# Moving the branch product of a stream-mixing layer from the autocorrelation's period into the last part of the kernel

## What is computed

```python
x_norm = x * jax.lax.rsqrt(jnp.mean(x * x, axis=-1, keepdims=True) + RMS_EPS)
H_res_logits = (x_norm @ W_res.T).reshape(B, T, n, n) + H_res_base
H_pre_logits = x_norm @ W_pre.T + H_pre_base
H_post_logits = x_norm @ W_post.T + H_post_base
H_res = sinkhorn_log(H_res_logits)          # 50 iterations on 4 x 4
H_pre = jax.nn.softmax(H_pre_logits, axis=-1)
H_post = jax.nn.softmax(H_post_logits, axis=-1)
H_res = (1.0 - g) * I + g * H_res
x_streams = x.reshape(B, T, n, C)
x_pre = jnp.einsum('btnc,btn->btc', x_streams, H_pre)
y = x_pre @ W_branch
x_mixed = jnp.einsum('btij,btjc->btic', H_res, x_streams)
y_distributed = jnp.einsum('btc,btn->btnc', y, H_post)
return (x_mixed + y_distributed).reshape(B, T, nC)
```

## Time and profile before

| | us |
|---|---|
| median of 3 runs | 1248.21 (1247.65 to 1251.31) |
| the profiled execution | 1247.06 |
| its span | 1245.1 |
| the last part (mixing_phase), in the span | from about 1109.4 |
| PE busy | 1029.9 (83%) |
| DVE busy | 932.4 (75%) |
| ACT busy | 641.3 (52%) |
| POOL busy | 492.4 (40%) |
| table loads of ACT | 25 in all, 1.28 each |

### The profile page before, as it was taken

How to read it: one execution, slowest core, us unless ns; L and a number is a source line. 1 busy time by engine, 2 the same in 40 slices (tenths; PEclk the granted TensorE clock), 3 DMA queues, 4 the chain that set the end, 5 groups by cost and what they waited for, 6 DMA issues and landing times. The chain is left out here.

```text
span 1245.1 us, 23491 instructions
## 1 busy us (share of the span) xinstructions
PE 1029.9 (83%) x7928; PEld 781.0 (63%) x7928; DVE 932.4 (75%) x2818; ACT 641.3 (52%) x1827; POOL 492.4 (40%) x684
## 2 busy tenths in 40 slices
PE   5699999999999999999648999999887995615056
PEld 4577777787777777777436677767665663313034
DVE  6766787666678666666507778779998998897994
ACT  6434555544455544445516677778567655323133
POOL 2523443333343333344324666666565542201020
PEclk9799999999999999999679999999999997657578
DMA  9011011111101111110132123223222211139025
GB/s 377 25 42 57 19 57 57 57 57 40 45 28 57 57 57 57 40 41 19 58 120 85 68 83 117 89 77 123 73 81 81 73 39 38 43 120 332 0 56 131
DMA packets 47235, 95.72 MB, mean 77 GB/s; under 512 B 5952, under 2 KB 30400, under 8 KB 47168
## 3 DMA queue, kind: packets, MB, share of 16 engines
q1 hardware_dynamic: 47168, 94.91, 22.9%
HBM read 64.48 MB, written 27.26 MB: 74 GB/s over the span
## 5 line engine op out<-in xcount | busy, mean ns | idle before, releaser
L613 POOL TENSOR_TENSOR prob_G<-prob_G,rl 128x512 f32<-128x512 f32 x96 | 99.8, 1040 | 258.2 <-DVE rl L501 258.2
L383 ACT ACTIVATE prob_G<-prob_G,negm 128x128 f32<-128x128 f32 x384 | 148.8, 389 | 89.5 <-DVE negm L443 89.5
L244 PE MATMUL ps_qkv<-w_hi,xT_hi 128*128 128x512 f32 x384 | 156.7, 408 | 13.5 <-DVE prob_G L506 8.6
L245 PE MATMUL ps_qkv<-w_lo,xT_hi 128*128 128x512 f32 x384 | 151.4, 394 | 0.0
L246 PE MATMUL ps_qkv<-w_hi,xT_lo 128*128 128x512 f32 x384 | 151.2, 394 | 0.0
L316 PE MATMUL ps_qkv<-wo_hi,aT_hi 128*128 128x512 f32 x256 | 107.7, 421 | 0.0
L318 PE MATMUL ps_qkv<-wo_hi,aT_lo 128*128 128x512 f32 x256 | 102.1, 399 | 0.0
L317 PE MATMUL ps_qkv<-wo_lo,aT_hi 128*128 128x512 f32 x256 | 101.9, 398 | 0.0
L244 PEld LDWEIGHTS ps_qkv<-w_hi,xT_hi 128*128 128x128 f32 x384 | 73.2, 191 | 39.0 <-issue 16.1
L439 DVE TENSOR_TENSOR prob_G<-ps_s,mask 128x512 f32<-128x512 f32 x96 | 65.0, 677 | 41.4 <-PE ps_s L227 40.8
L468 DVE TENSOR_TENSOR xT_lo<-ps_t,xT_hi 128x512 fp32r<-128x512 f32 x16 | 11.1, 693 | 104.2 <-ACT xT_hi L422 104.2
(11 more groups left out here) (246 smaller groups left out, 2819.6 us busy)
## 6 DMA issues: line engine op xcount, KB each, us to landing
xin<-in_x SPq DMA_DIRECT2D x16, 512.0 KB, 3.3
xres<-in_x SPq DMA_DIRECT2D x16, 512.0 KB, 5.0
x<-xres SPq DMA_DIRECT2D x16, 512.0 KB, 2.6
c_xin<-x SPq DMA_DIRECT2D x16, 512.0 KB, 4.9
c_cin<-in_ctx SPq DMA_DIRECT2D x16, 512.0 KB, 4.2
c_b_xres<-x SPq DMA_DIRECT2D x16, 512.0 KB, 3.3
rows_x<-c_row SPq DMA_DIRECT2D x64, 128.0 KB, 2.3
m_xm<-rows_x SPq DMA_DIRECT2D x16, 512.0 KB, 8.6
```

Of the source, the lines that this page charges most:

```text
L244: nc.tensor.matmul(ps_qkv[:, n, :], xT_hi[:, k, :], w_hi[:, k, cols], start=k == 0, stop=False)
L245: nc.tensor.matmul(ps_qkv[:, n, :], xT_hi[:, k, :], w_lo[:, k, cols], start=False, stop=False)
L383: r = nc.scalar.activation(prob(g)[:, j, :], prob(g)[:, j, :], ACT.Exp, bias=negm[:, h:h + 1], accum_out=lsum[:, h:h + 1])
L613: nc.gpsimd.tensor_tensor(prob(g), prob(g), rl[:, g * GROUP:(g + 1) * GROUP].rearrange("p (j o) -> p j o", o=1).to_broadcast([P, GROUP, T] ...
```

## The change

In the period of the autocorrelation the maxima, exponentials, reciprocals, the weighted sum, its transposes, the branch product and body 17 go; rows_x is sent as soon as x3 is there, and rows_y is not used. Chains b and c stand at steps 96 and 8, not 126 and 16, when the last part begins. In the last part DVE does the softmax of all 16 rows at once, on 128 x 16 x 8 values, between the steps of the chains, with one exponential on ACT. PE spreads the pre shares and the means (early), ACT copies them, and POOL builds diagonal tiles for all rows in four operations (pre_diag). Then a row's branch is eight products of 128x128 parts of the row with 32-column diagonal tiles, which give the transposed weighted sum, a copy by ACT, two products with W_branch, and a copy by ACT into ym. Branches of rows 0 to 4 come before chain a's output, those of rows 5 to 15 after it. At the kernel's start ACT asks for one table set that holds exponential and logarithm. The diff, cut:

```diff
 def attention_phase(...):
...
         def _(act):
+            nc.scalar.preload_act_table_set("natural_log_exp_and_others")
             act.wait_ge(const_in, 48)
...
 def advance(dve, chain, to, most=1000):
...
-        if k > 1:
+        if k == 1:
+            dve.wait_ge(chain.logits_done, chain.first_row + chain.n)
+        else:
             dve.wait_ge(chain.step, k - 1)
...
 def autocorrelation_phase(...):
...
-                         (15, 4): ((one_b, 56),), (16, 0): ((one_b, 88),), (16, 3): ((one_c, 2),), (16, 4): ((one_b, 100), (one_c, 6)),
-                         (17, 0): ((one_b, 116),), (17, 4): ((one_b, 126), (one_c, 16))})
+                         (15, 4): ((one_b, 56),), (16, 0): ((one_b, 86),), (16, 3): ((one_c, 2),), (16, 4): ((one_b, 96), (one_c, 8))})
...
-            body(B + 1, 1, near=False, far=False, last=False, tail=True, ahead=False)
...
-                if tail:
-                    sp.wait_ge(y_done, b - 1)
+                if last:
+                    sp.wait_ge(x3_done, b)
...
-                    sp.dma_start(rows_y[b - 2], row[par][:, D:ROW]).then_inc(row_out[par], 16)
...
-                    for i in range(2):
-                        r = nc.tensor.transpose(xpT_at[:, i * T:(i + 1) * T], xp[:, i * P:(i + 1) * P], idf[:])
-                    r.then_inc(xpT_ps, 1)
...
-                        r = nc.tensor.matmul(y_ps_at, xpT[:, i, :], wb_sb[:, i, :], start=i == 0, stop=i == 1)
...
-                    nc.scalar.activation(he[:], fact(b - 1, 1 - par, AT_PRE, NS), ACT.Exp, bias=hx[:, 0:1],
-                                         accum_out=hs[:, 0:1]).then_inc(he_done, 1)
...
-                        nc.vector.scalar_tensor_tensor(xp[:], x[:, n * C:(n + 1) * C], he[:, n:n + 1], xp[:], ALU.mult, ALU.add).then_inc(xp_step, 1)
...
 def mixing_phase(...):
...
+        pre_parts = ((0, 5), (5, 9), (9, 13), (13, 16))
...
         def _(pe):
             pe.wait_ge(const_in, 32)
+            pe.wait_ge(share_step, SHARES)
+            for g in range(NS):
+                r = nc.tensor.matmul(p_sel[:, g, 0:B * EARLY], sel_sb[:, g, :],
+                                     early[:, :, :].rearrange("p b k -> p (b k)"), start=True, stop=True)
+            r.then_inc(early_ps, 1)
+
+            def branch(n):
+                if n == 0:
+                    pe.wait_ge(wb_in, 16)
+                pe.wait_ge(pre_diag_done, 1 + max(i for i, (first, _) in enumerate(pre_parts) if n >= first))
+                if n > 0:
+                    pe.wait_ge(pre_done, n)
+                for h in range(2):
+                    for g in range(NS):
+                        r = nc.tensor.matmul(p_pre[:, h * T + g * W:h * T + (g + 1) * W], xm[n][:, g, h * P:(h + 1) * P],
+                                             pre_diag[:, n * NS + g, :], start=True, stop=True)
+                r.then_inc(pre_ps, 1)
+                pe.wait_ge(pre_done, n + 1)
+                if n > 0:
+                    pe.wait_ge(y_done, n)
+                for h in range(2):
+                    r = nc.tensor.matmul(p_y[:, 0:C], xpT[:, h, :], wb_sb[:, h, :], start=h == 0, stop=h == 1)
+                r.then_inc(y_ps, 1)
+
             for chain in chains:
...
+                if chain is not one_c:
+                    for c in chains[group(chain):(group(chain) + 1 if chain is one_a else len(chains))]:
+                        pe.wait_ge(rows_in[group(c)], 16 * c.n)
+                        for n in range(c.first_row, c.first_row + c.n):
+                            branch(n)
                 pe.wait_ge(coef_step, COEFS * (group(chain) + 1))
...
         def _(act):
...
+            def branch(first, to):
+                for n in range(first, to):
+                    act.wait_ge(pre_ps, n + 1)
+                    if n > 0:
+                        act.wait_ge(y_ps, n)
+                    nc.scalar.activation(xpT[:, :, :], p_pre[:, 0:2 * T].rearrange("p (h t) -> p h t", h=2), ACT.Copy).then_inc(pre_done, 1)
+                    act.wait_ge(y_ps, n + 1)
+                    nc.scalar.activation(ym[n][:], p_y[:, 0:C], ACT.Copy).then_inc(y_done, 1)
...
+            branch(0, 2)
+            logs(one_b, FIRST_LOGS + 1, FIRST_LOGS + BLOCK_LOGS)
+            branch(2, one_a.n)
             copies(one_a)
-            take_out(0, 2)
-            logs(one_b, FIRST_LOGS + 1, FIRST_LOGS + BLOCK_LOGS)
-            take_out(2, one_a.n)
+            take_out(0, one_a.n)
+            branch(one_b.first_row, one_b.first_row + 3)
             logs(one_c, FIRST_LOGS + 1, FIRST_LOGS + BLOCK_LOGS)
+            branch(one_b.first_row + 3, B)
             logs(one_b, FIRST_LOGS + BLOCK_LOGS + 1, FIRST_LOGS + 2 * BLOCK_LOGS)
...
         def _(pool):
             pool.wait_ge(const_in, 32)
+            pool.wait_ge(early_done, EARLY)
+            for first, to in pre_parts:
+                wide = [P, (to - first) * NS, W]
+                nc.gpsimd.tensor_tensor(pre_diag[:, first * NS:to * NS, :],
...
```

More of the change, by code:

```diff
@@ L765, in weave, with autocorrelation_phase @@
             advance(dve, chain, to, 1)
-def autocorrelation_phase(nc, x1, ctx_in, ident, dft, w24, base, wb, norm2, facts, chains, rows_x, rows_y):
+def autocorrelation_phase(nc, x1, ctx_in, ident, dft, w24, base, norm2, facts, chains, rows_x):
     with ExitStack() as ctx:
@@ L800, in autocorrelation_phase @@
         v_re, v_im = sb("v_re", [P, D]), sb("v_im", [P, D])
-        row = [sb(f"row{i}", [P, ROW]) for i in range(2)]
+        row = [sb(f"row{i}", [P, D]) for i in range(2)]
         tq = [sb(f"tq{i}", [P, D]) for i in range(2)]
@@ L1050, in body @@
                     weight_spectrum(p_c, 1)
-                if tail:
-                    pe.wait_ge(xp_step, XS * (b - 1))
+                if near and not far:
+                    pe.wait_ge(const_in, 64)
+                if near:
+                    correlate(0)
+                    correlate(1)
+                if last:
                     if far:
@@ L1055, in body @@
                     else:
-                        pe.wait_ge(x3T_done, 2 * (b - 1))
-                    for i in range(2):
-                        r = nc.tensor.transpose(xpT_at[:, i * T:(i + 1) * T], xp[:, i * P:(i + 1) * P], idf[:])
-                    r.then_inc(xpT_ps, 1)
[L1060 to L1066, removed]
-                        r = nc.tensor.matmul(y_ps_at, xpT[:, i, :], wb_sb[:, i, :], start=i == 0, stop=i == 1)
[L1068 to L1073, removed]
+                        pe.wait_ge(lg_done, b - 1)
                     pe.wait_ge(x3_done, b)
@@ L1400, in body, with mixing_phase @@
                     if last:
-                        pool.wait_ge(h_step, HS * (b - 1) + 1)
+                        pool.wait_ge(lg_done, b)
                     TT(rs[:], ms2[:], mhalf, ALU.pow).then_inc(rs_done, 1)
             iterations(pool, body)
-def mixing_phase(nc, rows_x, rows_y, facts, chains, gate, sel, fold, out):
+def mixing_phase(nc, rows_x, facts, chains, wb, gate, sel, fold, out):
     with ExitStack() as ctx:
@@ L1606, in _ @@
             left = BASES[1] - 2 - one_c.issued
-            weave(dve, (one_b, one_b.issued + left), (one_c, BASES[1] - 2))
+            both(left)
             advance(dve, one_b, one_b.issued + 3)
@@ L1679, in build @@
             first_row += n
-        autocorrelation_phase(nc, x1, ctx, ident, dft, w24, base, wb, norm2, facts, chains, rows_x, rows_y)
-        mixing_phase(nc, rows_x, rows_y, facts, chains, gate, sel, fold, out)
+        autocorrelation_phase(nc, x1, ctx, ident, dft, w24, base, norm2, facts, chains, rows_x)
+        mixing_phase(nc, rows_x, facts, chains, wb, gate, sel, fold, out)
 def rope_tables():
```

167 lines of the change are left out of this document (81 added, 86 removed).

## The result

| us | before | after |
|---|---|---|
| median of the runs of this comparison | 1248.28 | 1261.28 (1259.74 to 1264.89) |
| ratio, 95% interval | | 1.0103 (1.0076 to 1.0131) |
| profiled execution | 1247.06 | 1259.74 |
| its span | 1245.10 | 1257.90 |
| last part, from and length | 1109.4, 135.7 | 1076.3, 181.6 |

The changed kernel is 1.0% slower, as forecast (1260.0, slower at 0.56). Single executions of 1575 us (in the first experiment), 2631 us (in the pipelined one) and 4377 us (of the kernel before, beside the experiments) stand far outside all others, and the ratios are made without them.

The account below looks back on a forecast made before the run. TensorE bounds the early periods, VectorE with TensorE and ScalarE the late ones. 33.5 us saved starts the last part at 1075.9; its 182.1 (before 135.7) gives span 1258.0, plus 1.96: 1260.0 us. Range 1226 to 1270.

Parts of the forecast that it names:

- first load: Kernel start: preloading the first table set moves its load into idle time before; 1.0 us less, between 0 and 1.3.
- four periods: Four TensorE-bound periods after body 1: without transposes, branch product and wait each falls from 22.67 to 21.08; 6.3 us less.
- two periods: 807.35 to 856.28: two periods with four table loads fall from 48.93 to 43.0; 5.9 us less, at least 3.2.
- late periods: 856.28 to 1020.14: two table loads before body 11's copies go; 3.4 us less, from 0 to 9.
- body 14's x3 to the start of the last part: 1020.14 to 1109.40: 3.8 us less to body 15's end, 13.1 less in bodies 16 and 17.
- the terms 3 and 4: Gains from 807.35 to 856.28 (5.9 us) and from 856.28 to 1020.14 (3.4 us).
- Term 4: 856.28 to 1020.14: 3.4 us less from two table loads; VectorE's saving of about 1.6 a period counted at nothing, hidden.
- the row: Last part: each branch row takes 5.9 us at TensorE's low clock, 3.4 + 0.5 + 2.0, without overlap.
- The stalls: Last part: VectorE waits 18 us at chain c's first logarithms and 22 us at chain b's second ones.
- Rival (a): Last part: branch rows run at TensorE's high clock, 3.2 us each, so the kernel takes 1227.7 us; chance 0.20.
- the signs that I named: Profile: periods 21.1 to 21.4, one table load, 163.9 becoming about 160, last part from near 1076, low-clock rows, VectorE waits.

Follow-up runs that it names:

- the first experiment: Changed kernel with two idle 256-column matrix products added as fill to each branch row; 1240.6 us, ratio 0.9922 to the kernel before.
- the pipelined one: Changed kernel with TensorE doing the next branch row's narrow products before the current row's W_branch product; 1249.2 us, ratio 0.9993 to the kernel before.
- the version with the wait of 2.45: Changed kernel with idle products in each branch row, chain a's selection moved between branch rows 2 and 3, and ScalarE reordered; 1244.7 us, ratio 0.9967.
- One program: Changed kernel with three idle VectorE operations added in each of bodies 7 to 12; four executions took 1236.5, 1261.7, 1265.1 and 1234.6 us.

## Why the prediction held, step by step

Ahead of the last part, forecast and measured: first load 1.0 and 0.8; four periods 6.3 and 6.15; two periods 5.9 and 5.43; late periods 3.4 and 3.91; body 14's x3 to the start of the last part 3.8 + 13.1 = 16.9 and 16.8. Together 33.5 and 33.1; the last part began at 1076.3 and not 1075.9. The 0.8 may be chance: kernels with the request for the table set reach their first x3 between 694.09 and 696.40, those without it at 695.44 and 695.60. What the terms 3 and 4 did not separate, the table set's own experiment does: of the 5.43 some 3.3 come from the loads and 2.2 from TensorE's work that left, and of the 3.91 about 2.9 and 1.0. Term 4 counted VectorE's saving at nothing; 1.0 by this difference, and 2.1 to 2.4 of 7.2 in the experiment that put such work back, are not nothing, but most of it is hidden.

In the last part, from its start: the row is 5.80 (forecast 5.9), chain b's logarithms at 27.2 (28.4), chain a's last branch row done at 43.3 (44.6), chain c's logarithms at 80.1 (82.7), behind row 15 126.5 (128.2), chain b's first output row 133.4 (135.4), the end 181.6 (182.1). The stalls are 16.95 (18) and 23.95 (22). So the step that carries the sign, that the branch rows run at the low clock, held in all ten executions by their times.

That the last part came out within half a microsecond (182.1 and 181.6) is partly luck. Three errors made the forecast late: chain b was at its step 1.2 sooner (2.7 was set for VectorE beside GpSimd, and four slowed operations cost 2.0), each row was taken 0.1 too long, 1.2 in all, and selection and first diagonal took up to 0.8 less. Two made it early. The sum took row 8's narrow products as done behind chain c's logarithms (1.3 + 2.4). TensorE had begun them only at 1155.86, half a microsecond before those logarithms, and ScalarE waited for them:

```profile
1155.86 3.46 PE L1462 MATMUL p_pre<-m_pre_diag,m_xm 128*128 128x32 f32 x16
...
1156.39 0.20 ACT L719 ACTIVATE chain_c_lra<-chain_c_ra 128x12 f32<-128x12 f32 x1
...
1159.36 0.38 ACT L1528 ACTIVATE m_xpT<-p_pre 128x256 f32<-128x256 f32 x1 [1.76 <-PE p_pre L1462]
```

So row 8 cost a whole row and the logarithms nothing, 1.6 to 1.7 more than the sum had. And chain b's output took 27.7 us up to ScalarE's free point and not 25.5: I had carried over 25.5 "as before", but its first two rows now took 3.78 and 3.69, where the earlier trace rows has 3.39 and 1.97. That is the largest term that was mis-sized. It does not come from the low branch rows ahead: with all rows high the first two output rows took 3.78 and 3.72 as well (the version with chain c's logarithms behind row 8), and with low rows ahead 3.29 and 1.97 (ScalarE's order alone). Why the clock rises sooner in one execution than in another stays open. Rival (a)'s chain has a slip too: from 30.3 its rows give some 38 and 43 and not 40.0 and 43.6, though the 61.8 behind them is right to 0.3.

The argument behind 5.9 was right in its result and too simple in its form. It read from L1090 that such records don't raise the clock. They don't lower it by themselves either: plain rows held the high clock for 33 us once they had it. The prediction's "TensorE comes to row 5 at the high clock", which stood under rival (a), was the open point, and the changed kernel lost the clock in row 5's product (in both profiled executions), in the passage from output rows to branch rows and not in a later row. Rival (a) was therefore nearer than its row of evidence made it look: two idle products away, 1232.7 us against the 1227.7 worked out for all rows high (rows 0 to 4 stay low there).

The pipelined rows kept TensorE busy for 46.2 of 46.2 us, and the granted clock stayed at 0.50. The Trainium skill's rule (TensorE: Matmul & The Clock Gate, Part 1), that activity releases the clock, would have given 1228 as the prediction read it; the rows do not bear it out.

A table load took 1.28 us and stands between two activations with 0.02 on each side, in the kernel before:

```profile
1134.12 0.21 ACT L720 ACTIVATE chain_b_lcb<-chain_b_cb 128x32 f32<-128x32 f32 x1
1134.35 1.28 ACT L720 ACT_TABLE_LOAD   x1
1135.65 0.31 ACT L720 ACTIVATE chain_b_mat<-chain_b_logm 128x128 f32<-128x128 f32 x1
```

The drain of about 1.38 per switch that the Trainium skill adds (ScalarE: Activation LUTs, What ACT_TABLE_LOAD costs) doesn't show here, and the experiment on the table set came out at 1233.9 and not at the 1222 to 1227 that a drain was to give.

Of the signs that I named, one table load, 160.0, 1076, and VectorE without a wait at chain b's first logarithms are there. The periods were 21.1 to 21.3 up to 800 us; the next two, up to 844, took 21.9 and 21.6, over the 21.4 that was named. The waits of 16.95 and 23.95 stand for 18 and 22.

## What to carry to other kernels

When work moves out of a TensorE-bound loop to a place where TensorE idles, price it at the clock of that place: here 1.6 us a row were saved in the loop and 5.8 a row paid behind it. Before giving up such a move, look at how the clock is entered and lost: here a wait of 2 to 3 us on TensorE, or the passage from one kind of row to another, decided between 3.3 and 5.8 us for every row that followed (3.7 and 6.8 with idle products in it), and two idle products at that place were worth some 25 us. Idle time on an engine is no gain in store: look where it goes when its cause is removed. And split a change with two parts: one table set alone on the kernel before gave 1.1%, and the other part hid it.

## What the runs showed of the hardware

- The granted clock has a memory. The same mix, TensorE busy all the time, ran at 1.00 for 14 us and at 0.50 for 48 us in one execution, with a wait of 2.45 us between.
- Plain branch rows sustain either level: 3.31 apart at 1.00, 5.80 apart at 0.50. Removing the gap in a row did not raise it; idle products did in one place (from row 0 to row 1 of the fill experiment) and not in others (rows 3 and 4 of the same experiment, behind a wait of 3.23, and row 8 on in the version with the wait of 2.45).
- One program took 1235 or 1262 to 1265 us, at mean granted clocks of 0.92 to 0.93 or 0.90. The changed kernel, with the same rows, was at the low level in ten of ten. What makes the difference, chance, the 2 us by which the last part is shifted or the added VectorE operations, stays open. Nor is it shown whether the two idle products in row 5 hold the clock by what they are or by the time that they take: no other filling was tried.
- Behind high branch rows, TensorE's wait of 2.49 us for chain b's coefficients was followed by a selection of 1.97 to 2.07 in three profiled executions and of 1.16 in one, and the wait of 2.63 by a first output row of 3.57 to 3.78 in all four. With idle products in these waits the two took 1.16 and 1.99, and 1225.0 became 1220.6 us.
